# Giving runs of block products a place by unit instead of by couple in a graph-network kernel

## The reference

```python
# layer 0: relational graph convolution, 8 bases
msg = sum_b (h[src] @ weight[b]) * w_comp[etype][:, b];  msg = msg * norm
x1  = layernorm(x + relu(segment_sum(msg, dst) + bias))
# layer 1
neigh = segment_sum(x1[src] + edge_attr, dst)
h   = ((1 + eps) * x1 + neigh) @ W1 + b1            # 128 -> 256
h   = relu(batchnorm(h) * gamma + beta)
out = layernorm(x1 + h @ W2 + b2)
```

## Time and profile before

| | us |
|---|---|
| median of 3 runs | 603.48 (603.25 to 607.04) |
| the profiled execution: its time | 605.07 |
| its span | 603.3 |
| PE busy | 507.7 (84%) |
| VectorE (DVE) busy | 458.3 (76%) |
| POOL busy | 401.1 (66%) |
| ScalarE (ACT) busy | 218.0 (36%) |

### The profile page before, as it was taken

The page is one execution under the profiler, slowest core; times in us unless marked ns, Lnnn a source line. Parts: engine busy times, 40 slices in busy tenths (PEclk is TensorE's granted clock), DMA queues, the critical chain, the costliest instruction groups (busy, mean ns, idle before and its releaser), DMA issues.

```text
span 603.3 us, 12767 instructions
## 1 busy us (share of the span) xinstructions
PE 507.7 (84%) x3965; PEld 429.8 (71%) x3965; DVE 458.3 (76%) x1811; ACT 218.0 (36%) x323; POOL 401.1 (66%) x434
## 2 busy tenths in 40 slices
PE   4769888986868968878968899878899799899995
PEld 2459888776767657766757786767779699778775
DVE  6999999999885888877599887788844555527466
ACT  9904544453333242333333333422400000003276
POOL 5777777777777777777777777777777777720000
PEclk9986676997777996779997989978979899899999
DMA  5423756675664674665675868656667775843003
GB/s 131 123 55 93 246 187 181 208 258 167 195 199 139 205 229 141 200 216 197 193 242 185 269 166 292 178 196 212 227 195 234 221 225 153 265 127 109 3 2 107
DMA packets 98456, 108.18 MB, mean 179 GB/s; under 512 B 10949, under 2 KB 84918, under 8 KB 98386
## 3 DMA queue, kind: packets, MB, share of 16 engines
q1 hardware_dynamic: 79394, 77.81, 39.3%
q0 software_dynamic: 13312, 27.29, 16.0%
q10 hardware_dynamic: 5680, 2.23, 1.5%
HBM read 81.73 MB, written 25.56 MB: 178 GB/s over the span
## 4 chain that ended last, share of the span: by engine, by line
PE 47%; DVE 22%; DMA 17%; issue 5%; POOL 5%; SPq 1%; ACT 1%; DVEq 1%; POOLq 0%; ACTq 0%
PE psum L1218 16%; DMA gathered_flat<-in_x_dram,src_i 14%; PE psum L1135 10%; PE psum L1193 7%; DVE etype_hot L1610 5%; POOL gathered_flat L829 5%; PE psum L1128 5%; PE psum L1159 4%; DVE etype_hot L1607 3%; DVE sums_flat L1738 3%; DVE weighted L1495 2%; DVE adj_flat L1467 2%; DMA sums_flat<-in_x_dram 2%; PE psum L1361 2%; PE psum L1384 1%
## 5 line engine op out<-in xcount | busy, mean ns | idle before, releaser
L829 POOL DMA_INDIRECT gathered_flat<-in_x_dram,src_i x416 | 398.8, 959 | 129.8 <-issue 90.2
L914 ACT ACTIVATE adj_flat<-psum 128x500 f16<-128x500 f32 (+1 forms) x208 | 127.4, 612 | 236.0 <-PE psum L1159 226.7
L1135 PE MATMUL psum<-weighted,gathered_flat 128*128 128x96 f32 (+1 forms) x832 | 150.7, 310 | 39.5 <-DMA gathered_flat<-in_x_dram,src_i 39.4
L1135 PEld LDWEIGHTS psum<-weighted,gathered_flat 128*128 128x128 f32 x832 | 129.7, 218 | 45.0 <-DMA gathered_flat<-in_x_dram,src_i 44.9
L1128 PEld LDWEIGHTS psum<-hot,attrs 128*128 128x128 f32 x832 | 148.1, 217 | 12.3 <-issue 9.8
L1610 DVE TENSOR_SCALAR etype_hot<-iota_key,key_t 128x300 f16<-128x300 f16 (+1 forms) x416 | 136.0, 329 | 0.0
L1128 PE MATMUL psum<-hot,attrs 128*128 128x12 f32 (+1 forms) x832 | 133.2, 238 | 2.4 <-DVE weighted L1495 2.4
L1159 PE MATMUL psum<-etype_hot 128*128 128x300 f16 (+1 forms) x416 | 131.2, 344 | 2.5 <-DVE etype_hot L1610 2.5
L1607 DVE TENSOR_SCALAR etype_hot<-iota_key,gathered_flat 128x128 f16<-128x128 f16 x416 | 106.2, 255 | 22.3 <-PE psum L1159 15.5
L1738 DVE TENSOR_TENSOR sums_flat<-psum,sums_flat 128x180 f32 x208 | 71.1, 342 | 27.7 <-DVE sums_flat L1687 8.3
L1218 PE MATMUL psum<-sums_flat 128*128 128x264 f16 x630 | 83.7, 292 | 4.0 <-DVE weighted L1495 3.8
(11 more groups left out here) (158 smaller groups left out, 358.7 us busy)
## 6 DMA issues: line engine op xcount, KB each, us to landing
attrs<-in_edge_attr_dram SPq DMA_DIRECT2D x51, 512.0 KB
adjacency<-adj_flat SPq DMA_DIRECT2D x26, 900.0 KB
sums_flat<-adjacency SPq DMA_DIRECT2D x12, 576.0 KB, 5.5
gathered_flat<-in_x_dram,src_i POOLq DMA_INDIRECT x416
coef<-adjacency SPq DMA_DIRECT2D x21, 288.0 KB, 6.2
sums_flat<-adjacency SPq DMA_DIRECT2D x7, 432.0 KB, 5.5
sums_flat<-adjacency SPq DMA_DIRECT2D x10, 288.0 KB, 5.0
sums_flat<-adjacency SPq DMA_DIRECT2D x3, 504.0 KB, 8.5
```

Source lines behind the costliest of these rows:

```text
L829: pool.indirect_dma_start(gathered[:, t % (RING * GROUP), :], None, x[:, :], bass.IndirectOffsetOnAxis(src_i[:, t:t + 1], 0)).then_inc(gat ...
L914: nc.scalar.activation(window, counts, ACT.Copy).then_inc(counts_copied, 1)
L1135: nc.tensor.matmul(unit_psum(u)[:, 0:B, STARTS[i]:STARTS[i] + WIDTHS[i]], gathered[:, (u * UNIT + i) % (RING * GROUP), 0:F], weighted_tile ...
```

## The change

`run_bank_at(u)` gives a bank to a unit instead of a couple. For units whose number leaves 2 or 3 when divided by 4, nothing changes. From `SECOND` = 2 * 83 + 14 = unit 180 on, the units that leave 0 and 1 get a place too, on banks 4 and 5, which the counts no longer need. `plan_runs` walks over the units, and from unit 180 on the lead is one couple shorter. Nothing else is rewritten: the rest follows the plan. By the arithmetic of the planner there are then 62 runs with 276 source tiles instead of 50 with 262. The first 36 runs (up to unit 179) are the same. From unit 180 to 206 there are 25 runs with 96 tiles instead of 13 with 88; the one at unit 207 has 2 tiles instead of 6. The tail has 49 source tiles in 18 finals (10 in five, 39 in thirteen) instead of 63 in 19 (18 in six, 45 in thirteen). VectorE may now have two runs to add in a couple, and it loads the bases of both before the first.

```diff
--- before.py
+++ after.py
@@ -133,7 +133,7 @@
     RUN_TILES = CT * SPREAD
     FREE_COEF = -(-RUN_TILES // (GROUP * B))
     LEAD = 3
-    FILL_COUNT = 6
+    FILL_MOST = 6
 
     def split_step(k):
         return (AGG_AT[k] + TURN_AT + 3) // 4
@@ -151,18 +151,23 @@
             places = [(NEARS + FARS + i, (i + 1) * FREE_COEF - 2) for i in range(COEFS)] + places
         return places
 
-    def run_bank_of(w):
-        if w % 2 == 0:
+    SECOND = 2 * ALL_COUNTED + 14
+
+    def run_bank_at(u):
+        if u % 4 == 2:
             return 7
-        if w > ALL_COUNTED:
-            return 3
-        held = any(first - 2 <= 2 * w + 1 <= at + KEEP_AT + 1 for first, at in zip(FIRST, AGG_AT))
-        return None if held else 6
+        if u % 4 == 3:
+            if u // 2 > ALL_COUNTED:
+                return 3
+            held = any(first - 2 <= u <= at + KEEP_AT + 1 for first, at in zip(FIRST, AGG_AT))
+            return None if held else 6
+        return 4 + u % 4 if u >= SECOND else None
 
     def plan_runs():
 
         runs, reached, used = [], [0] * BLOCKS, {}
-        for w in range(COUPLES):
+        for u in range(U):
+            w = u // 2 - (u + 1) % 2
             ready = sum(2 * w >= at + 2 * split + 3 for at, split in zip(AGG_AT, SPLIT))
 
             def most(b):
@@ -174,14 +179,14 @@
             def tiles(b, parts):
                 return PART_AT[reached[b] + parts] - PART_AT[reached[b]]
             b = max(range(BLOCKS), key=lambda b: (tiles(b, most(b)), -b))
-            if run_bank_of(w) is None:
+            if run_bank_at(u) is None:
                 continue
             for parts in range(most(b), 0, -1):
                 steps = [(max(opens, -(-used.get(place, 0) // 2), block_step(b)), i, place)
                          for i, (place, opens) in enumerate(places_for(tiles(b, parts)))]
                 step, _, place = min(steps)
-                if 2 * step + 2 + LEAD <= w:
-                    runs.append((w, b, reached[b], reached[b] + parts, place, step))
+                if 2 * step + 2 + LEAD - (u >= SECOND) <= w:
+                    runs.append((u, b, reached[b], reached[b] + parts, place, step))
                     reached[b] += parts
                     used[place] = w
                     break
@@ -191,6 +196,7 @@
     NRUNS = len(RUNS)
     RUN_AT = {run[0]: n for n, run in enumerate(RUNS)}
     LAST_RUNS = [(b, PART_AT[REACHED[b]]) for b in range(BLOCKS)]
+    FILL_COUNT = min(FILL_MOST, sum(first < PART_AT[LOOPED] for _, first in LAST_RUNS))
     FILLED_BLOCKS = sorted(sorted(range(BLOCKS), key=lambda b: (LAST_RUNS[b][1], b))[:FILL_COUNT])
 
     def spaced(blocks, chosen):
@@ -211,7 +217,7 @@
     assert all(first < last for _, first, last in FINALS) and len(FINALS) == FILL_COUNT + BLOCKS
     FINAL_BANKS = (7, 1, 4, 6, 5, 3)
     EARLY_LOADS = 4
-    assert U % RU == 0 and run_bank_of(COUPLES - 1) == FINAL_BANKS[-1]
+    assert U % RU == 0 and run_bank_at(U - 1) == FINAL_BANKS[-1]
     HALF_CHUNK = CHUNK // 2
     LAST_CHUNK = (CHUNKS - 1) * CHUNK
     PIECES = ((0, HALF_CHUNK), (HALF_CHUNK, HALF_CHUNK)) + tuple((k * CHUNK, CHUNK) for k in range(1, CHUNKS - 2))
@@ -232,14 +238,18 @@
     assert SETTLED + 2 < BLOCKS
 
     def run_bank(n):
-        return run_bank_of(RUNS[n][0])
+        return run_bank_at(RUNS[n][0])
 
     def final_added(n):
 
         return BLOCK * NRUNS + min(BLOCK * n + 3, BLOCK * len(FINALS))
 
-    def runs_before(w):
-        return sum(run[0] < w for run in RUNS)
+    def runs_of_couple(w):
+
+        return [n for n, run in enumerate(RUNS) if (run[0] + 1) // 2 == w]
+
+    def runs_added(w):
+        return sum((run[0] + 1) // 2 <= w for run in RUNS)
 
     def run_uses(n):
         return [m for m in range(n) if RUNS[m][4] == RUNS[n][4]]
@@ -696,7 +706,7 @@
                         sp.wait_ge(adj_out[i], 16 * (b + 1))
 
                 def load_run(n):
-                    w, b, first, last, place, step = RUNS[n]
+                    at, b, first, last, place, step = RUNS[n]
                     stored(b)
                     if place >= NEARS + FARS:
                         sp.wait_ge(select_ready, (place - NEARS - FARS + 1) * FREE_COEF)
@@ -1227,16 +1237,16 @@
                     return [(h, counts[:, :, h - at, :]) for h in range(first, last)]
 
                 def run_products(n):
-                    w, b, first, last, place, step = RUNS[n]
+                    at, b, first, last, place, step = RUNS[n]
                     pe.wait_ge(run_in[place], 16 * (len(run_uses(n)) + 1))
                     pe.wait_ge(parts_ready, last)
                     before = [m for m in range(n) if run_bank(m) == run_bank(n)]
                     if before:
                         pe.wait_ge(nbr_added, BLOCK * (before[-1] + 1))
                     if run_bank(n) == 7:
-                        pe.wait_ge(select_ready, min(w // 2 + 2, GROUPS))
+                        pe.wait_ge(select_ready, min((at // 2 - 1) // 2 + 2, GROUPS))
                     if run_bank(n) == 6:
-                        pe.wait_ge(x1_kept, sum(start <= 2 * w for start in FIRST))
+                        pe.wait_ge(x1_kept, sum(start <= at - 1 for start in FIRST))
                     if run_bank(n) < 6:
                         pe.wait_ge(counts_copied, U)
                     first, last = PART_AT[first], PART_AT[last]
@@ -1251,7 +1261,7 @@
                             pe.wait_ge(added, done_unit(k))
                             if k:
                                 pe.wait_ge(x1_kept, k)
-                            own_bank = [m for m in range(runs_before(u // 2)) if run_bank(m) == 6]
+                            own_bank = [m for m in range(NRUNS) if RUNS[m][0] < u and run_bank(m) == 6]
                             if own_bank:
                                 pe.wait_ge(nbr_added, BLOCK * (own_bank[-1] + 1))
                         each = B // PART_TILES[k]
@@ -1261,9 +1271,8 @@
                             turn_back(k)
                         if u == AGG_AT[k] + TURN_AT:
                             turn_norm(k)
-                    w = u // 2 if u % 2 else u // 2 - 1
-                    if w in RUN_AT and u < U - 1 and (run_bank_of(w) == 7) == (u % 2 == 0):
-                        run_products(RUN_AT[w])
+                    if u in RUN_AT and u < U - 1:
+                        run_products(RUN_AT[u])
 
                 def final_products(n):
                     b, first, last = FINALS[n]
@@ -1287,7 +1296,7 @@
                 bases(LOOPED, 0, B)
                 for k in LATE:
                     turn_back(k)
-                if COUPLES - 1 in RUN_AT:
+                if U - 1 in RUN_AT:
                     run_products(NRUNS - 1)
                 for n in range(FILL_COUNT):
                     final_products(n)
@@ -1710,26 +1719,25 @@
                     g = 2 * w // GU
                     if w % 2 == 0:
                         places = group_values(g, 0, N - 1)
-                    if w - 1 in RUN_AT:
-                        firsts = block_bases(RUNS[RUN_AT[w - 1]][1])
+                    runs = runs_of_couple(w)
+                    firsts = {n: block_bases(RUNS[n][1]) for n in runs}
+                    pending = [(n, j) for n in runs for j in range(BLOCK)]
                     for k in range(LOOPED):
                         if w == AGG_AT[k] // 2 + OWN + 1:
                             dve.wait_ge(own_added, k + 1)
-                    run = RUN_AT.get(w - 1)
-                    added_of_run = 0
                     for c in range(min(U, counted(2 * w - 2) + KEYRING), min(U, counted(2 * w) + KEYRING)):
                         keys_hot(c)
-                        if run is not None and added_of_run < BLOCK:
+                        if pending:
                             dve.wait_ge(added, 2 * w)
-                            add_run(run, added_of_run, firsts)
-                            added_of_run += 1
-                    if run is not None:
+                            n, j = pending.pop(0)
+                            add_run(n, j, firsts[n])
+                    if pending:
                         dve.wait_ge(added, 2 * w)
-                        for j in range(added_of_run, BLOCK):
-                            add_run(run, j, firsts)
+                        for n, j in pending:
+                            add_run(n, j, firsts[n])
                     dve.wait_ge(sums_mm, w + 1)
-                    if run is not None:
-                        dve.wait_ge(nbr_added, BLOCK * runs_before(w))
+                    if runs:
+                        dve.wait_ge(nbr_added, BLOCK * runs_added(w))
                     for j in range(2):
                         u = 2 * w + j
                         window = sums[:, :, bass.ds(places[u % GU], WIN)]
```

## The result

| | us | ratio to before |
|---|---|---|
| before, 20 runs beside those of after | 604.75 (602.3 to 607.75) | |
| after, 20 runs | 610.21 (604.66 to 612.34) | 1.0079 [1.006, 1.0099] |
| the profiled execution of after | 608.81, span 607.0 | |

The change costs 0.8%, some 4.8 us. I had said 603.8, with a range up to 608.6. The median of before is 1.3 us higher in this larger number of runs than the one I started from; that explains a small part of the miss, the rest is in the kernel.

The account below looks back on a forecast made before the run. VectorE's queue was to end the loop, with the shorter tail paying it back: loop +2.3, bases +2.2, tail -4.2 us, together +0.3 on the 603.48 median, so 603.8 us, range 598.0 to 608.6.

Parts of the forecast that it names:

- PE's side: Loop: 54 matmuls moved in from the tail, 6.1 us, fit into 10.4 us of PE's waits and slow clock.
- the 537.3 I had as a floor: Loop end: unit 207 done no earlier than 537.3, from last gather at 531.00, 5.59 us landing and 0.7 us more.
- VectorE in the loop: Last couples: more runs' adds and register loads end the loop at 540.9 against 538.57, +2.3 us.
- The bases: Sixteen matmuls behind the loop, 4.43 us before, run partly at 1.2 GHz after PE's wait: +2.2 us, bounds 0 and 4.4.
- the two losses of the earlier trace: Kernel before: slow clock behind PE's 3.50 and 2.42 us idles lost 1.7 and 2.8 us; used to cost the bases.
- Start of the full finals: Tail: PE waits for VectorE's split and the last run's two adds, 0.5 us, so they start at T + 6.4.
- T: End of the late nodes' transposes behind the loop, 544.21 before; the tail's times are counted from it.
- The full finals: Tail: 39 tiles, 117 matmuls at 0.113 us, 13.2 us, ending at T + 19.6; tail -4.2 us.
- The sum: Whole kernel: 2.3 + 2.2 - 4.2 = +0.3 us on the median of 603.48, so 603.8.
- The loads of the tail: Tail: block 11's counts come at about T + 4.5, costed at nothing; as a rival, late loads give 606.1, chance 0.07.
- VectorE keeps up: Rival, loop: register loads hide behind the adds, loop ends at the gathers' floor: 597.9 to 598.9, chance 0.20.
- The clock stays down: Rival, from unit 203 on: slow clock in loop, bases and first tail tiles, +5.4 to +7.4: 608.9 to 610.9, chance 0.13.

Follow-up runs that it names:

- adds_before: Kernel before, with only VectorE given one more pair of base loads and two unused adds in twelve couples, no product moved: ratio 1.0101 to the kernel before.
- once_after: Changed kernel with the 26 block bases loaded into VectorE's registers once ahead of the loop instead of two per run: ratio 0.9985 to the kernel before.
- split_after: Changed kernel with one register load per base, two per run (124 loads instead of 62): ratio 1.0103 to the kernel before.
- warm_after: Changed kernel with 45 more matmuls, results unused, on PE behind unit 207 while it waits for VectorE: ratio 1.0089 to the kernel before.
- bank2_after: Changed kernel with bank 2 in place of bank 3 as the sixth bank of the final products: ratio 1.0049 to the kernel before.
- min4: Changed kernel with no run of fewer than 4 tiles from unit 180 on: ratio 0.9987 to the kernel before.

## Why the prediction was wrong, step by step

- **PE's side: right.** No wait at unit 182, full clock there, the room for the 54 matmuls was found. PE ended unit 207 at 535.50, 1.8 us before the 537.3 I had as a floor: the last gather started at 531.11, and PE didn't have to wait the 5.59 us that I had given it. It didn't matter, since VectorE ends the loop.
- **VectorE in the loop: right, its number partly by luck.** I had 540.9 for the end of its adds, by start at 513.2 and steps of 7.4, 3.84, 3.42, 3.84, 4.5, 3.84. It was 540.84, with a start at 512.60 and steps of 7.36, 4.22, 3.42, 3.86, 4.69, 3.86. The start was 0.6 us earlier and the steps together 0.6 us longer than I had: that the sum agrees to 0.1 us is luck. adds_before shows that this work is enough by itself, and the time of once_after that without the loads the loss is gone.
- **The bases: too low by 0.75 us.** I took the middle of the two losses of the earlier trace rows, +2.2; it was +2.95. With 5.40 us idle, longer than either of the two idle times there, the granted clock was 0.50 (1.2 GHz) for the first 4.1 us, eight of the sixteen. Of the two losses the larger, 2.8 us, was the nearer; the upper bound, all at half, was not reached.
- **Start of the full finals: too early by 0.8 us.** T + 7.19 for T + 6.4. The split ended at T + 5.84, as said. The two adds of the last run I had at 0.5 us together, by the close adds of the earlier trace rows; here they took 1.16 us, with 0.59 us between them, 0.42 of which the chain calls "issue", time without a visible cause (timeline of VectorE, after):

```profile
555.20 0.28 DVE L1696 TENSOR_TENSOR sums_flat<-psum,sums_flat 128x132 f32 x1
556.07 0.29 DVE L1696 TENSOR_TENSOR sums_flat<-psum,sums_flat 128x132 f32 x1 [0.59 <-DVE sums_flat L1696]
```

- **The full finals: 1.7 us not in the sum at all.** This is the step that failed. I had 117 matmuls at 0.113, 13.2 us, the rate of a PE that hadn't waited. But by my own working PE waits before them, and I had charged the clock for the wait before the bases and not for this one. Behind the 2.00 us wait the clock was 0.71 over the first 5.8 us: 36 matmuls took 5.88 us, and not the 4.22 us of the kernel before. once_after, split_after and warm_after have the same 5.88 us behind waits of 1.51 to 2.02 us; bank2_after, with the wait cut in two, has 4.37. Not every such wait does it: min4 had full clock behind 1.76 us, and what decides is not shown. The tail gave back 1.6 us in place of 4.2.
- **The sum.** 0.75 + 0.8 + 1.7 = 3.3 us on top of +0.3 make +3.6; the two spans differ by 3.7. The timed runs say about 4.8, with 3.6 to 6.0 as the interval. The median of after, 610.21, stands 6.4 us above my 603.8: 1.3 of them are the median of before, 3.4 are in the stages above, and the other 1.7 are in no stage of this one profiled execution. Where they arise stays open.
- **The loads of the tail:** the counts of block 11 cost PE 0.55 us at 553.36, hidden as costed; its late issue is seen in SyncE's queue, 550.20 where the earlier trace rows has 536.62:

```profile
550.20 0.90 SPq L740 DMA_DIRECT2D coef<-adjacency  x2
```

- **The rivals.** VectorE keeps up: no; once_after is what it would have looked like. The clock stays down: in part. From unit 203 on it was at full speed in one profiled execution and at half in the other, and of that rival's terms the bases paid a third (0.75 of 2.2 us beyond my forecast) and the first tiles of the tail 1.7 of 1 to 3. That the measured time lies in its range, 608.9 to 610.9, doesn't make its mechanism right. I had made one case of it, all or nothing, with 0.13. But each of its three terms hangs on a wait of its own, and two of these waits were in my forecast itself. The Trainium skill, "TensorE: Matmul & The Clock Gate", section "HAM oscillation — how this bites in real kernels", says that the engine is throttled again at each burst behind a long wait. The trace agrees for the waits of 5.40 and 2.00 us (0.50 and 0.58 behind them), and not for those of 1.61 and 1.14 us in the loop, behind which the matmuls ran at full rate; nor for the 1.76 us of min4. I had quoted the rule and then not applied it to the second wait.

## What to carry to other kernels

Cost a piece of work on each engine in that engine's own unit: here PE pays per tile and VectorE per run, and splitting about the same tiles (96 for 88) over twice the runs filled PE's gaps and took VectorE's. A scalar that an engine's queue reads from memory stands in that queue like an instruction; where that queue is what ends the loop, read it once ahead of it (the kernel before, where it isn't, gained nothing). And whenever the working says that PE waits, ask at once for the clock behind that wait, at every such place: in the profiled execution the matmuls behind the two waits cost 2.95 and 1.7 us, twice the 2.3 us of the late loop.
